# Gated cross-attention and LoRA experts: a reordered prelude, and the first five samples' scores through four PSUM banks

## What is computed

```python
Q = split_heads(layernorm(x)) * 8 ** -0.5
K, V = split_heads(ctx[..., :128]), split_heads(ctx[..., 128:])
logits = Q @ K.T + b - 1e12 * (key >= seq_len[sample])
x = x + tanh(g_xattn) * (softmax(logits) @ V)
# eight experts with a shared 128 -> 512 -> 128 MLP and LoRA of rank 16 each;
# the two with the best gate scores are taken
x = x + tanh(g_ffn) * experts(layernorm(x))
```

## Time and profile before

| | |
|---|---|
| three runs, median | 277.94 us (277.12 to 278.81) |
| the profiled execution | 278.2 us, span in the trace 276.4 us |
| PE busy | 245.5 us (89% of the span) |
| DVE busy | 214.0 us (77%) |
| ACT busy | 163.0 us (59%) |
| POOL busy | 158.5 us (57%) |
| DMA | 23.46 MB, mean 85 GB/s |
| chain that ended last | PE 57%, DVE 24%, POOL 5%, ACT 5%, issue 5% |

### The profile page before, as it was taken

One profiled execution on the slowest core, in us unless ns is written; L12 is line 12 of the kernel. 1 busy time (PEld: TensorE's weight loads), 2 busy tenths in 40 slices (PEclk: granted clock), 3 DMA queues, 4 the chain that ended last, 5 costly groups with the idle time before them and its releaser, 6 DMA issues.

```text
span 276.4 us, 8038 instructions
## 1 busy us (share of the span) xinstructions
PE 245.5 (89%) x2966; PEld 184.3 (67%) x2966; DVE 214.0 (77%) x623; ACT 163.0 (59%) x319; POOL 158.5 (57%) x306
## 2 busy tenths in 40 slices
PE   0368979899998999989999979999999999999895
PEld 0135556566665566656567658888888989897865
DVE  4778786899999999997949999858585858585432
ACT  5778785889897989896877642333334242323220
POOL 6888676687877786686892447090919250505120
PEclk9999999999999999999999999999999999999999
DMA  4749997736776866640000000101010101001011
GB/s 110 202 124 209 208 222 181 206 83 196 178 215 160 215 160 162 149 71 6 8 6 2 4 0 0 39 2 38 0 40 0 42 0 30 10 7 31 2 38 38
DMA packets 48461, 23.46 MB, mean 85 GB/s; under 512 B 7680, under 2 KB 48296, under 8 KB 48424
## 3 DMA queue, kind: packets, MB, share of 16 engines
q1 hardware_dynamic: 47520, 22.77, 34.5%
q10 hardware_dynamic: 904, 0.19, 0.4%
HBM read 7.29 MB, written 2.10 MB: 34 GB/s over the span
## 4 chain that ended last, share of the span: by engine, by line
PE 57%; DVE 24%; POOL 5%; ACT 5%; issue 5%; DMA 2%; ACTq 1%; POOLq 0%
PE bank L1102 21%; DVE negmax L1313 11%; PE bank_max L1137 10%; PE bank L1012 7%; PE bank L1044 5%; PE bank L1079 2%; DVE rest L1264 2%; PE bank L1055 2%; PE bank L1095 2%; PE bank L1018 2%; DMA b_rows<-in_L_xattn_b_dram 2%; DVE hsum L1440 2%; ACT stack L760 2%; DVE KV L1326 1%; PE bank L1068 1%
## 5 line engine op out<-in xcount | busy, mean ns | idle before, releaser
L1313 DVE TENSOR_REDUCE negmax<-bank 128x4 f32<-128x512 f32 x128 | 83.3, 680 | 10.7 <-PE bank L1012 10.6
L809 ACT ACTIVATE probs<-bank 128x512 f32<-128x512 f32 x128 | 71.7, 602 | 15.0 <-PE bank L1018 13.9
L1012 PE MATMUL bank<-stack 64*128 64x128 bf16 x512 | 51.9, 235 | 9.6 <-DVE negmax L1313 6.0
L1012 PEld LDWEIGHTS bank<-stack 64*128 64x128 bf16 x512 | 31.7, 101 | 31.2 <-DVE negmax L1313 19.8
L1102 PE MATMUL bank<-u_part,b_part 128*128 128x512 f32 x192 | 52.0, 399 | 0.1
L849 ACT ACTIVATE h<-bank,bi_col 128x512 f32<-128x512 f32 x32 | 22.1, 690 | 49.4 <-PE bank L1102 49.4
L1018 PE MATMUL bank<-stack 64*128 64x128 bf16 x512 | 48.5, 223 | 0.3
L1440 DVE SCALAR_TENSOR_TENSOR hsum<-bank,nbi_col,h 128x512 f32<-128x512 f32 x32 | 23.9, 748 | 24.0 <-PE bank L1102 24.0
L648 POOL TENSOR_TENSOR x_part<-KV,x_part 128x512 fp32r<-128x512 f32 x8 | 10.4, 1301 | 55.8 <-ACT x_part L831 55.8
L1044 PE MATMUL bank<-probs,vpad 128*32 128x128 f32 x1024 | 42.1, 283 | 0.0
L1102 PEld LDWEIGHTS bank<-u_part,b_part 128*128 128x128 f32 x192 | 35.5, 189 | 8.3 <-ACT h L849 0.5
(11 more groups left out here) (136 smaller groups left out, 407.0 us busy)
## 6 DMA issues: line engine op xcount, KB each, us to landing
stack<-part SPq DMA_DIRECT2D x96, 128.0 KB, 3.0
KV<-in_ctx_dram SPq DMA_DIRECT2D x5, 512.0 KB, 4.1
X<-in_x_dram SPq DMA_DIRECT2D x7, 256.0 KB, 4.3
out_dram<-res SPq DMA_DIRECT2D x7, 256.0 KB, 2.3
KV<-in_ctx_dram SPq DMA_DIRECT2D x5, 256.0 KB, 5.6
stack<-bias_line SPq DMA_DIRECT2D x7, 48.0 KB
stack<-max_rows SPq DMA_DIRECT2D x13, 24.0 KB
X<-in_x_dram SPq DMA_DIRECT2D x2, 128.0 KB, 2.4
```

What stands on the lines that cost most here:

```text
L809: act.activation(probs[:, i % 4, :], sc2[i % 2][:, :], ACT.Exp).then_inc(s_exp, 1)
L1012: mm = pe.matmul(sc1[i % 2][:, j * 128:(j + 1) * 128], stack[at, s, h0 + 2 * j, q0:q0 + 128], stack[at, s, h0 + 2 * j, 512 + q0:640 + q0], ...
L1313: dve.tensor_reduce(negmax[:, p % 2, n % 2, 8 * (u // 2) + u % 2:8 * (u // 2) + u % 2 + 7:2], bank_cols(sc1[i % 2]), AX.X, ALU.max, negate ...
```

## The change

Part one, the prelude:

- On ACT's queue `b_rows` is issued first, then one of the three copies of `seq_len` (`seq_col`), then `seq_row`; the two other copies go to SP, between `load_k(0)` and `load_x(1)`.
- POOL's sum with `b_rows` becomes a step of its own (`bias_add`), behind `bias_places`.
- The transfer of line 0 into the stack moves from SP to ACT's queue, right behind `copy_line(0)`.
- Line 2 is placed by PE before the loop and copied by ACT in the prelude, instead of after unit 2 of sample 0; PE's transposes of pair 2 move behind the first two units of sample 0.
- DVE: pair 0's rest comes before the moments of samples 2 and 3, and its third part before `scale(1)`.

Part two, samples 0 to 4 (`ALONE = LAG`): pass one goes through banks 0 to 3, unit c of each sample in bank c, in the order of units 2, 0, 3, 1. PE issues two units at a time, one matmul of the upper half and one of the lower in turn. The first unit of a group waits for the maxima of the group two before it. Pass two's first units wait for the last maxima that read banks 2 and 3.

```diff
-        LINE_AT = {(0, 0, 2): 2, (0, 1, 2): 3, (1, 0, 1): 4, (1, 1, 0): 5, (1, 1, 3): 6, (2, 0, 1): 7}
+        LINE_AT = {(0, 1, 2): 3, (1, 0, 1): 4, (1, 1, 0): 5, (1, 1, 3): 6, (2, 0, 1): 7}
+        ALONE = LAG
+        UNITS1_ALONE = (2, 0, 3, 1)
+        def unit1(m, c):
+            return UNITS1_ALONE[c] if m < ALONE else UNITS1[c]
+        def first_bank(m, c):
+            return bank[c] if m < ALONE else sc1[c % 2]
 SP
             load_k(0)
+            for i in range(1, PARTS):
+                sp.dma_start(seq_col[B * i:B * (i + 1), :], seq_len).then_inc(s_col, 16)
             load_x(1)
...
             pair_to_stack(0, 1)
-            bias_to_stack(sp, 0)
             pair_to_stack(0, 2)
 POOL
             bias_sum()
             bias_places()
+            bias_add()
             bias_split()
 ACT
-            for i in range(PARTS):
-                act.dma_start(seq_col[B * i:B * (i + 1), :], seq_len).then_inc(s_col, 16)
+            act.dma_start(b_rows[:, :], b.rearrange("(o k) -> o k", o=1).to_broadcast([PARTS * B, S])).then_inc(s_b, 16)
+            act.dma_start(seq_col[0:B, :], seq_len).then_inc(s_col, 16)
             act.dma_start(seq_row[:, :], seq_len.rearrange("b o -> o b").to_broadcast([128, B])).then_inc(s_seq, 16)
-            act.dma_start(b_rows[:, :], b.rearrange("(o k) -> o k", o=1).to_broadcast([PARTS * B, S])).then_inc(s_b, 16)
...
             copy_line(0)
+            bias_to_stack(act, 0)
             normalise_first(1)
...
             bias_to_stack(act, 1)
+            copy_line(2)
             load_gates()
 PE
+            def scores_alone(m, c):
+                i, p, s, q0 = CH * m + c, m // 2, (m // 4) % SLOTS, (m % 4) * 128
+                if c == 0 and m % 2 == 0:
+                    pe.wait_ge(s_stack[p % len(s_stack)], stack_done(p))
+                if i == 2:
+                    pe.wait_ge(s_rest, LEAD)
+                if i >= 4:
+                    pe.wait_ge(s_max, i - 2)
+                for j in range(G):
+                    for k in range(2):
+                        at, h0 = score_rows(unit1(m, c + k))
+                        mm = pe.matmul(first_bank(m, c + k)[:, j * 128:(j + 1) * 128], stack[at, s, h0 + 2 * j, q0:q0 + 128],
+                                       stack[at, s, h0 + 2 * j, 512 + q0:640 + q0], start=True, stop=True)
+                        if j == G - 1:
+                            mm.then_inc(s_sc1, 1)
...
-                    if k == 0:
-                        pe.wait_ge(s_rest, LEAD)
+                    if k < 2:
+                        pe.wait_ge(s_max, CH * ALONE - 1 + k)
...
             place_bias(1)
-            transpose_k(2)
-            transpose_q(2)
+            place_bias(2)
...
-                        scores(m, n, c)
+                        if m >= ALONE:
+                            scores(m, n, c)
+                        elif c % 2 == 0:
+                            scores_alone(m, c)
+                        if (q, i, c) == (0, 0, 0):
+                            transpose_k(LEAD)
+                            transpose_q(LEAD)
 DVE
+            first_rest(0)
             moments_of(1)
-            first_rest(0)
+            third_part(0)
             scale(1)
-            for n in range(4, 6):
-                stats_of(n)
-            third_part(0)
-            for n in range(6, 8):
+            for n in range(4, 8):
                 stats_of(n)
```

More of the change, by code:

```diff
@@ L530, in bias_sum, with bias_add @@
                                    ALU.mult).then_inc(s_bias, 1)
+            def bias_add():
                 pool.wait_ge(s_bias, 1)
@@ L1010, in scores @@
                     if first:
-                        (at, h0), q0 = score_rows(UNITS1[c]), (m % 4) * 128
-                        mm = pe.matmul(sc1[i % 2][:, j * 128:(j + 1) * 128], stack[at, s, h0 + 2 * j, q0:q0 + 128],
+                        (at, h0), q0 = score_rows(unit1(m, c)), (m % 4) * 128
+                        mm = pe.matmul(first_bank(m, c)[:, j * 128:(j + 1) * 128], stack[at, s, h0 + 2 * j, q0:q0 + 128],
                                        stack[at, s, h0 + 2 * j, 512 + q0:640 + q0], start=True, stop=True)
@@ L1311, in row_max @@
                     dve.wait_ge(s_msplit, NMS * (p - 2) + 2)
-                u = UNITS1[c]
-                dve.tensor_reduce(negmax[:, p % 2, n % 2, 8 * (u // 2) + u % 2:8 * (u // 2) + u % 2 + 7:2], bank_cols(sc1[i % 2]), AX.X, ALU.max,
+                u = unit1(n, c)
+                dve.tensor_reduce(negmax[:, p % 2, n % 2, 8 * (u // 2) + u % 2:8 * (u // 2) + u % 2 + 7:2], bank_cols(first_bank(n, c)), AX.X, ALU.max,
                                   negate=True).then_inc(s_max, 1)
```

## The result

The changed kernel takes 279.56 us in the median of 7 runs (278.65 to 279.94), the kernel before, in 7 runs beside it, 278.13. The ratio is 1.0049, 95% interval 1.0028 to 1.0069: slower by 0.5%. The prediction said 276.2, faster. The profiled execution took 279.07, with a span of 277.3 (before: 278.2 and 276.4). Here and in the experiments the medians are of all runs, and the ratios of the runs in the fast state alone, so a ratio need not be the quotient of two medians.

The account below looks back on a forecast made before the run. It took ACT's queue to set the hand-over into the steady part. Gains of 0.25 (prelude), 1.04 (four banks) and 0.45 (line 7) summed to 1.74 us, giving a median of 276.2 us, range 274.5 to 277.9.

Parts of the forecast that it names:

- B: Rival: gain eaten on ACT by line 0's issue, late `seq_col` or late pair 1; gain 0.9 us, 277.0, chance 0.24.
- Two `seq_col` loads on SP: Prelude: SP's later loads start at most 1.6 us later, nothing on the path waits for them; cost nothing.
- b_rows first: Prelude: bias chain on POOL ends 1.44 us earlier unless `seq_col` is late; mostly spent on ACT, counted as 0.25.
- pair 1's moments also move behind the first rest on DVE: Prelude, DVE's order: given as a reason why later x and keys of samples 2 and 3 cost nothing.
- Line 0 issued on ACT: Prelude: issue priced at 1.37 us on ACT's queue ahead of pair 1's normalisation, which starts at 11.9 to 12.4.
- Four banks: First five samples: PE no longer waits for two banks, so q(4) starts when POOL is done; gain 1.04 us.
- ACT idle at line 7: Before the first exp: PE places line 7 before ACT asks, so ACT's idle time goes; gain 0.45 us.
- the unseen bound: Landing of pair 1's stack transfers, not shown in the trace; at worst q(4) at 26.9, a gain of 0.6 us.
- Upper and lower in turn: First five samples' scores: saves 6.5 us of PE time beside the path; counted nothing, at most 3.4 us.
- A: Rival: the clock rises earlier in the work, one sample less at the low level saves 1.2 us; 275.0, chance 0.13.
- C: Rival: the clock rises later in the work, three more samples at the low level add 3.6 us; 279.8, chance 0.06.

Follow-up runs that it names:

- e11: The changed kernel with `b_rows` last on ACT's queue again, the two `seq_col` loads still on SP; 279.57 us, ratio 1.0065.
- e3: The changed kernel with all four loads (`seq_col`, `seq_row`, `b_rows`) issued on ACT as in the kernel before; 277.85 us, ratio 0.9971.
- e13: e11 with the two `seq_col` loads on SP ahead of the first K tile's load instead of behind it; 277.87 us, ratio 0.9986.
- e4: The changed kernel with all three `seq_col` loads on ACT's queue, `b_rows` still first there; 279.69 us, ratio 1.0046.
- e5: e3 with line 0's transfer issued by SP again instead of ACT; 276.90 us, ratio 0.9974.
- e9: e1 with one line moved on POOL, so `bias_add` comes behind `bias_places`; no loads moved; 275.48 us, ratio 0.9917.
- e6: e1 with the two units of a pair one after the other instead of upper and lower in turn; 277.33 us, ratio 0.9961.
- e1: The changed kernel with the prelude and loads of the kernel before, so part two of the change alone; 276.47 us, ratio 0.9948.
- e7: e1 with ACT's last fill of stack slot 3 moved from before the first exp to four places later; 276.33 us, ratio 0.9933.
- e8: e1 with unread extra matmuls on PE: 23 in the prelude's idle time, two ahead of each score group; 277.50 us, ratio 0.9994.

## Why the prediction was wrong

By the prediction's own sign it was wrong as in B: the first maximum is not earlier. What failed is the prelude, which was to gain 0.25 and lost 2.43: two steps were put at nothing (the loads on SP, DVE's order), one price was left out (`b_rows` first), and one was taken too low (line 0).

- *"Two `seq_col` loads on SP ... Cost nothing"* is the first step that failed. It asked only what these loads hold up, and not what holds them up. In the changed kernel they land 4.0 us after their issue, in e11 5.0, against 2.3 on ACT in e3; the place behind K alone shifts the first maximum by 2.46 (e11 against e13). Rival B named `seq_col`, but priced the whole of its losses at 0.84.
- *"b_rows first ... the bias chain ends 1.44 earlier (no wait is left in it), unless `seq_col` comes late."* The wait went away, the condition came true, and its price had been left out of the sum. With 48 KB in front, x, `seq_col` and `seq_row`, which are all wanted sooner, come later. Alone it costs 1.25 (e4 against e3); with the loads on SP, 1.72. The Trainium skill, page "DMA: Bandwidth & Descriptors", section "Issuing engines are not separate DMA queues", says that transfers end up on the same DMA engines and interleave, whoever issues them. This agrees with x on SP's queue coming 0.91 later once `b_rows` leads ACT's (3.98 against 3.07). The next section of this page of the Trainium skill, "Two DMAs through the same engine are not ordered", says that the descriptors of one queue on one DMA engine start in order. The 5.0 against 3.0 us on SP's queue agree.
- *"pair 1's moments also move behind the first rest on DVE"* stood in the prediction as a reason for no cost. It is the second step put at nothing: these moments lead to `qadd`, which pair 1's normalisation waits for. The normalisation was said to start when line 0 is copied and issued, at 11.9 to 12.4; `qadd` was left out of it. The first maximum is 1.06 later with it (e5 against e9), about 0.9 of that by the order, which takes nearly all that the split sum gains.
- *Line 0 issued on ACT, 1.37*: it took 1.58, and costs 0.68 at the first maximum (e3 against e5). Mis-sized, not wrong in kind.
- *The gain in the wait for `b_rows`* was real: e9, which takes it with the split sum alone, moves the first maximum 1.03 ahead of before and 0.95 ahead of e6.
- *Four banks 1.04, ACT idle at line 7 0.45*: right. From the first maximum to q(4) there were 8.57 us and are 7.53, which is the 1.04; between the two landmarks 1.53 was measured, and e1 gained 1.4 us in time. The landing of pair 1's parts, the unseen bound, did not bite: q(4) follows POOL.
- *Upper and lower in turn, nothing*: right (e6).
- *Rivals A and C, the clock.* In pairs of scores the pitch falls from 0.10 to 0.05 after 46.6 in the changed kernel and at 45.6 before. That is 1.1 later with work that is 0.9 later, so neither A nor C explains the result. C's time, 279.8, is near the measured one by chance: its cause did not come. In e9 the pitch is still 0.10 at 43.1, 6.1 behind the first exp as in the changed kernel, and 0.06 at 43.65. The rise moved with the work, and e9's gain of 2.57 at the first exp is kept whole in the span (2.7).

A sum of the steps as measured, at the first maximum: split sum -1.03 (before to e9), DVE's order with the early line 2 +1.06 (e9 to e5), line 0 on ACT +0.68 (e5 to e3), both load moves +1.72 (e3 to the changed kernel), which is +2.43 in the prelude; then -1.53: +0.90. The steps are differences of single executions. The first starts from the kernel before, whose first maximum is known to 1 us only.

## What to carry to other kernels

When a load is moved, ask both ways: what it delays, and what it will now stand behind, by the size of what is in front; a few bytes that many engines wait for go ahead of the first large tile. Before a load is moved forward because someone waits for it, try to move the waiting instruction back: it cost one line here, and was worth more than the change it came from. When a step is moved back in one engine's order because something else is wanted sooner, follow what the step leads to: here the moments led to `qadd`, and moving them cost about what the split sum gained. A landmark reached earlier isn't yet time: of three kernels with the first exp 1 us earlier, two had lost it by the end of the attention.

## What the runs showed of the hardware

- Issuing line 0, `stack<-bias_line`, took ACT 1.51 to 1.62 and SP 0.93, and ACT's next compute instruction started only behind it. The first such issue on ACT is the dear one: where line 0 is issued there, line 1 takes 0.76 (e3, 17.48), and where it is not, line 1 takes 1.37.
- Instructions of DVE and POOL that ran at the same time took longer in the prelude. e9 differs from e1 in POOL's order alone: DVE's two normalisations took 0.70 in e1, where POOL waited for `b_rows` meanwhile, and 1.24 in e9, beside POOL's placement pattern. In the changed kernel, beside the same pattern (8.28 to 9.45), they took 1.51. Rows of DVE and POOL in e9, then of POOL in the changed kernel:
```profile
6.20 1.24 DVE L1289 TENSOR_SCALAR xhat<-X,mv,qmul 128x128 f32<-128x128 f32 x2
6.12 1.17 POOL L530 TENSOR_SCALAR_AFFINE_SELECT place<-place 96x192 bf16<-96x192 bf16 x1 [0.27 <-ACT place L770]
```
```profile
8.28 1.17 POOL L531 TENSOR_SCALAR_AFFINE_SELECT place<-place 96x192 bf16<-96x192 bf16 x1
```
POOL's mask took 1.18 in the changed kernel, where DVE filled a slot of `stack` from 6.94 to 7.62, and 0.72 in the kernel before (rows of POOL: changed, then before). No run moves this pair of instructions alone:
```profile
7.12 1.18 POOL L540 TENSOR_SCALAR mask_rows<-key_id,seq_colf 96x128 f32<-96x128 f32 x1 [1.22 <-DVE seq_colf L1318]
```
```profile
5.75 0.72 POOL L529 TENSOR_SCALAR mask_rows<-key_id,seq_colf 96x128 f32<-96x128 f32 x1 [0.18 <-POOL key_id L525]
```
- In e7's profiled execution PE stopped for 1.10 in the middle of a group of sixteen matmuls that waited for nothing in the profile. What it was isn't shown by a run of its own:
```profile
57.01 0.14 PEld L1075 LDWEIGHTS bank<-probs,vpad 128*32 128x32 f32 x4 [1.10 <-issue]
```
- Added matmuls can have the clock high early and still bring nothing: in e8 it was at the 1.2 GHz level again from 38.8 to 42.0, in work that PE filled without a gap, behind 2 us in which PE had waited for the first exp.
